# One-hots of five message blocks from one VectorE instruction in a graph layer with a mixture-of-experts layer behind it

## What is computed

```python
h_self = input @ W_self.T + b_self
H_all = jnp.einsum('rod,nd->rno', W_rel, input) + b_rel[:, None, :]   # 16 relations
msg_to_heads = H_all[rel, tails]
msg_to_tails = H_all[rel + R, heads]
agg = segment_sum(msg_to_heads, heads, N) + segment_sum(msg_to_tails, tails, N)
x = x + relu(h_self + agg)
x = x + experts(layernorm(x))
```

## Time and profile before

| what | value |
|---|---|
| median of 3 runs | 734.15 us (733.11 to 736.56) |
| the profiled execution's own time | 737.15 us |
| its span, first to last instruction | 735.4 us |
| mean granted TensorE clock | 0.98 |
| busy: TensorE, VectorE, ScalarE, GpSimd | 95%, 84%, 68%, 42% |

### The profile page before, as it was taken

One profiled execution on the slowest core, in us unless ns is written; L12 is line 12 of the kernel. 1 busy time (PEld: TensorE's weight loads), 2 busy tenths in 40 slices (PEclk: granted clock), 3 DMA queues, 4 the chain that ended last, 5 costly groups with the idle time before them and its releaser, 6 DMA issues. The chain is left out here.

```text
span 735.4 us, 10603 instructions
## 1 busy us (share of the span) xinstructions
PE 695.0 (95%) x3210; PEld 546.5 (74%) x3210; DVE 617.0 (84%) x1204; ACT 500.8 (68%) x717; POOL 307.4 (42%) x279
## 2 busy tenths in 40 slices
PE   4999989999998989999997899999999999999993
PEld 4777766777776767777765688888888888888882
DVE  8899978997997757777775899999998999999990
ACT  3555466774675757877556498888877888888860
POOL 3000077752777577776771033322234223333201
PEclk9999999999999999999999899999999999999997
DMA  8347588884988888997767989999999999999932
GB/s 244 124 143 270 176 264 293 302 273 149 305 288 275 268 288 273 302 310 211 226 203 252 353 318 349 398 407 394 401 369 369 367 402 372 363 395 372 371 106 29
DMA packets 54436, 212.75 MB, mean 289 GB/s; under 512 B 9753, under 2 KB 10150, under 8 KB 39158
## 3 DMA queue, kind: packets, MB, share of 16 engines
q1 hardware_dynamic: 34998, 153.85, 55.5%
q0 software_dynamic: 19392, 58.35, 27.3%
HBM read 184.36 MB, written 27.80 MB: 289 GB/s over the span
## 5 line engine op out<-in xcount | busy, mean ns | idle before, releaser
L400 POOL DMA_INDIRECT rows_sb<-h_dram,row_of x190 | 210.9, 1110 | 170.4 <-DVE row_of L544 83.8
L554 DVE TENSOR_TENSOR rows_lo<-rows_sb,rows_hi 128x512 fp32r<-128x512 f32 x175 | 119.8, 685 | 53.6 <-ACT rows_hi L692 53.3
L825 PE MATMUL p_h<-g_hi_sb,xt_hi_whole 128*125 128x512 f32 x320 | 129.6, 405 | 1.1 <-ACT p_h L686 0.8
L826 PE MATMUL p_h<-g_lo_sb,xt_hi_whole 128*125 128x512 f32 x320 | 127.6, 399 | 0.0
L827 PE MATMUL p_h<-g_hi_sb,xt_lo_whole 128*125 128x512 f32 x320 | 127.5, 398 | 0.0
L692 ACT CAST rows_hi<-rows_sb 128x512 fp32r<-128x512 f32 x175 | 99.2, 617 | 29.3 <-DMA rows_sb<-h_dram,row_of 27.1
L677 ACT COPY h_whole<-p_h 125x512 f32<-125x512 f32 x80 | 46.9, 586 | 89.9 <-PE p_h L827 89.9
L1190 POOL DMA_INDIRECT tokens<-token_dram,rows_of_tokens x15 | 21.7, 1444 | 171.2 <-ACT rows_of_tokens L1479 131.9
L859 PE MATMUL p_sum<-rows_hi,seg_hot 128*125 128x512 f32 x175 | 72.7, 416 | 8.6 <-DVE rows_lo L554 8.2
L1243 DVE TENSOR_TENSOR u_lo_sb<-stage_up,u_hi_sb 128x2048 fp32r<-128x2048 f32 x34 | 76.4, 2285 | 1.0
L1243 DVE TENSOR_TENSOR d_lo_sb<-stage_down,d_hi_sb 128x2048 fp32r<-128x2048 f32 x32 | 71.8, 2286 | 3.1 <-ACT d_hi_sb L1464 3.0
(11 more groups left out here) (291 smaller groups left out, 1308.8 us busy)
## 6 DMA issues: line engine op xcount, KB each, us to landing
stage_up<-in_L_ffn_up_w SPq DMA_DIRECT2D x34, 1024.0 KB, 8.2
stage_gate<-in_L_ffn_gate_w SPq DMA_DIRECT2D x32, 1024.0 KB, 8.7
stage_down<-in_L_ffn_down_w SPq DMA_DIRECT2D x32, 1024.0 KB, 7.7
h_dram<-h_whole SPq DMA_DIRECT2D x80, 224.0 KB
stage_up<-in_L_gnn_W_rel SPq DMA_DIRECT2D x16, 1024.0 KB, 8.0
x_whole<-in_L_gnn_b_rel SPq DMA_DIRECT2D x16, 256.0 KB, 9.5
rows_sb<-h_dram,row_of POOLq DMA_INDIRECT x190, 4.9
h_dram<-h_whole SPq DMA_DIRECT2D x80, 26.0 KB
```

The lines of the kernel that those rows point to most:

```text
L400: q.indirect_dma_start(rows_sb[:, b % ROWS], None, h_dram[0:1 + made(n) * TP], bass.IndirectOffsetOnAxis(ap=row_of[:, b:b + 1].bitcast(U32 ...
L554: v.tensor_tensor(rows_lo[:, b % PARTS], rows_sb[:, b % ROWS], rows_hi[:, b % PARTS].bitcast(F32), ALU.subtract).then_inc(part_lo, 1)
L825: m.matmul(o, xt_hi[:, dc, at], wt_hi_sb[:, 1 - j % 2, dc], start=(by_matmul and dc == 0), stop=False, skip_group_check=True)
L826: m.matmul(o, xt_hi[:, dc, at], wt_lo_sb[:, 1 - j % 2, dc], start=False, stop=False, skip_group_check=True)
```

## The change

The one-hots of blocks b to b + 4 are made ahead of block b, where b is a multiple of five, by one `tensor_tensor` that compares `seg_iota` (the same 125 numbers for each of five blocks) with `seg_of` (one number for each block, the same for 125 elements): 625 elements a lane. It waits for `block_done` of b - 5. Nothing else is moved.

```diff
+            assert last_span % HOT == IN_DIR[0] % HOT == HOTS % HOT == 0
...
                 def message(b):
-                    if b >= HOTS:
-                        dve.wait_ge(block_done, b - HOTS + 1)
-                    v.tensor_scalar(seg_hot[:, b % HOTS], seg_iota[:], seg_of[:, b:b + 1], None, ALU.is_equal)
+                    if b % HOT == 0:
+                        if b >= HOTS:
+                            dve.wait_ge(block_done, b - HOTS + HOT)
+                        v.tensor_tensor(seg_hot[:, b % HOTS:b % HOTS + HOT], seg_iota[:].unsqueeze(1).to_broadcast([P, HOT, TP]),
+                                        seg_of[:, b:b + HOT].unsqueeze(2).to_broadcast([P, HOT, TP]), ALU.is_equal)
                     dve.wait_ge(part_hi, b + 1)
```

## The result

The kernel after takes 746.32 us (median of 4 runs, 745.16 to 751.02), the kernel before beside it 734.22 us: a ratio of 1.0172, 95% interval 1.0134 to 1.0209. It is slower, outside the range, and by the mechanism of the first rival. The profiled execution has a span of 743.3 us, 7.9 us over that of before.

A forecast was written before the change was run, and what follows sets the result against it. TensorE was taken to set the products' pace and GpSimd's gathers the messages' end. Terms -0.6 - 0.4 + 0.2 = -0.8 us gave 736.35 from the profiled 737.15, or 733.3 for the median; range 728 to 744.

The forecast's parts named there:

- the first rival: Gathers wait behind a run of low parts, 0.60 us per second wait: slower, 744 to 745 us, chance 0.25.
- What bounds the kernel: TensorE sets the products' pace, 4.17 us a late step; GpSimd's gathers set the messages' end; VectorE is one step behind TensorE.
- (c): End of the messages: three new one-hots, blocks 160, 165 and 170, beside gathers; +0.2 to +0.6 us, +0.2 taken.
- VectorE's gain: 35 wide one-hots replace 175 small ones: 35 - 25.2 = 9.8 us of VectorE's time, 14 to 1.4 at the ends.
- (a): TensorE's wait at 231 us for the last chunk of columns: three one-hots of 0.20 us go, -0.6 us.
- (b): TensorE's wait at 273 us: how early GpSimd issues gathers; between -1.4 and +1.4 us, -0.4 taken.
- The low parts' delay: One low part in five comes up to 0.52 us later; 18 us without cover, expected hidden by VectorE's idle time.

The follow-up runs named there:

- e8: The change made for blocks 90 to 174 alone, with blocks 0 to 89 keeping the one-hot of the kernel before; ratio 1.0008 to the kernel before.
- e7: Kernel after with a one-element `tensor_scalar` added ahead of every low part of blocks 0 to 89; ratio 1.0010 to the kernel before.
- e1: Kernel after with five old `tensor_scalar` one-hots, grouped ahead of every fifth block, in place of the wide one; ratio 1.0178 to the kernel before.
- e2: Kernel before with each block's one-hot made by its own `tensor_tensor` of 125 elements, in the same place; ratio 1.0307 to the kernel before.
- e14: Kernel after with a 170-element `tensor_scalar`, constant scalar, ahead of every low part of blocks 0 to 89; ratio 1.0408 to the kernel before.
- e17: Kernel after with a `tensor_reduce` of 125 elements ahead of every low part of blocks 0 to 89; ratio 1.0143 to the kernel before.
- e15: Kernel after with a 170-element `tensor_scalar`, one scalar per lane, ahead of every low part of blocks 0 to 89; ratio 1.0081 to the kernel before.
- e13: Kernel after with the low parts of blocks 0 to 89 as `scalar_tensor_tensor` with a lane scalar; ratio 1.0150 to the kernel before.

## Why the prediction was wrong

**What bounds the kernel** held: the late steps are 4.17 us, the wait for the columns fell away, and gathers 150 to 189 take 397.24 - 344.93 = 52.3 us, 51.8 before; of (c)'s 0.2 to 0.6 us it is 0.5.

**VectorE's gain** was right in its main term, 0.807 us a record and 0.72 from the one-hot's start to the low part's (124.80 - 124.08), and 7.2 us less busy against 9.8 said. Nothing shows that it bought time: e8, with 17 of the 35 wide one-hots and no spacer, is at 1.0008. e7 can't tell, since its spacers take back some 6 us of the gain.

**(a)** went further than -0.6: the wait for the columns, 2.07 us, is gone, and the stretch at 231 us has clock 1.00, not 0.51. The time that the change saves VectorE did not do it: in e1 and e2, which save nothing, the step that took 8.42 us takes 5.14 and 4.65. What did stays open. It is tempting to put it to the 16 us by which the rest was late, but e14 is 28.2 us late there and its step takes 8.34, and e8, whose code is that of before up to block 90, takes 6.42. So part of this gain is the scatter of one stall from execution to execution.

**(b) is the step that failed.** It said that a gather which meets a `tensor_tensor` is longer by part of that one, put what all gathers together do to the time between -1.4 and +1.4 us, and took -0.4. The first 90 alone grew by 15.7 us. The price of a second wait in the first rival, 0.60 us, was right for one, and was counted as if a second were all. A run is waited through to its end, 0.60 by 0.60 with 0.80 for the new one-hot, up to six. The rival had them in three steps of ten; long ones came nine times in 90, at 2.3 to 4.3 us. Its time of 744 to 745 came close to 746 by luck, as a sum of other terms: fewer waits, each two to five times dearer, none in late steps, and 8 us got back.

**The evidence against the rival** was one gather. At 140.28 a second instruction had started at 140.61 and the gather didn't wait for it; at 144.71 one did. Both were read as a coin that falls either way. The trace of before had the difference, a few lines ahead of those in rows 10:

```profile
138.40 0.69 DVE L554 TENSOR_TENSOR rows_lo<-rows_sb,rows_hi 128x512 fp32r<-128x512 f32 x1 [0.54 <-ACT rows_hi L692]
```

VectorE had been idle until 138.40, 2.3 us before the low part at 140.01 ends. At 144.71 it had worked for 6.8 us without a gap. The count above puts the first among the cases that go either way and the second among those that wait, and beside the columns two of three are of the second kind.

What I did not ask was why no gather of before was over 1.89 us when VectorE is busy 19.28 of 20 us. In the steps neighbours of that kind stand at most two deep, so a wait could hardly be longer: the trace had no room to show the new case. The rule of the Trainium skill that I weighed said which instructions contend, and I used it for how many meet, not for how long they stand side by side.

**Bounds and chances.** The low parts' delay, 18 us without cover, did not show: e7 has it and loses nothing. Slower had 0.25; the trace of before did not exclude the price of a run, so more was due to it.

## What to carry to other kernels

Where GpSimd gathers beside a busy VectorE, look at what stands between VectorE's two-operand instructions before merging or moving it. Look there where VectorE is behind; where it comes out of idle time every few instructions, no wait was long. A cheap instruction can be the only opening that the gathers have, and its place is then worth more than its time: compare e2 (same VectorE time, 3.1% slower) with e7 (90 instructions more, loss gone). Read the gathers by their longest, not by their mean, and ask what the order of before made impossible to see.

## What the runs showed of the hardware

- A gather that is waiting when a VectorE instruction with two SBUF operands ends is mostly not let in if the next one of its kind follows at once (records overlap by 0.08 us) and VectorE has worked without a gap for at least 2.19 us: with eight instructions or more behind it, 381 of 439 had to wait on, and with fewer than four none of 517. Up to six were waited through, 4.33 us. It ends 0.81 to 0.83 us after the run (0.89 to 0.90 where the last one is a column's second half). The Trainium skill (SBUF — State Buffer, Who interferes with whom) says that two SBUF inputs contend with a GpSimd instruction that reads SBUF, and that the holder has the port pair for its whole instruction. The traces agree, and go further: the hold outlasts the instruction. Why the time without a gap matters stays open.
- What opens a run: an instruction of one element, a reduction of 125, and a `tensor_scalar` with a lane scalar (125 or 170 elements): 202 of 202. What mostly doesn't: a `tensor_scalar` of 170 elements with a constant, 13 of 55. The same section says that `tensor_scalar` in a mode with two ports contends as well, and that `tensor_reduce` never does on trn2; e14 and e17 agree. By it e15's and the old one-hot would contend like e14's, which the prediction left out, and both let gathers in at their start. The two kinds have nearly the same rate (e15's 304 ns for 170 elements and the old one-hot's 280 for 125 are 0.53 ns an element, e14's 245 and e7's 147 for one are 0.58), so the 59 ns are spent apart from the elements. That the gather goes in during them fits, and is argued, not shown.
- A lane scalar on a two-operand instruction opens a run about every other time (e13, 19 of 41), too seldom to help. That stays open too.
